# Linear attention fused with its fetch and norm: 64-token scores on array tiles in place of prefix sums

## The reference

```python
# x: (2, 2048, 128); 16 heads of 8 channels
q, k, v = (x @ Wq.T + bq), (x @ Wk.T + bk), (x @ Wv.T + bv)   # split into heads
kv = cumsum(k[..., :, None] * v[..., None, :], axis=tokens)   # an 8x8 state per head
o = einsum("d,de->e", q, kv)                                  # per token and head
x = layernorm(x + o @ Wo.T + bo)
logits = x @ Wr                                               # 8 experts
```

## Time and profile before

| | |
|---|---|
| median of 3 runs | 961.96 us (959.95 to 966.99) |
| span of the profiled execution | 962.4 us |
| fetch, from the first gather, to the start of the attention's own work | 514.8 to 558.0 us |
| attention, first projections and first pieces | 558.0 to 568.9 us |
| attention, from there to its last piece | 568.9 to 697.7 us |
| norm n2 with the router | 697.7 to 729.3 us |

### The profile page before, as it was taken

The page is one execution under the profiler, slowest core; times in us unless marked ns, Lnnn a source line. Parts: engine busy times, 40 slices in busy tenths (PEclk is TensorE's granted clock), DMA queues, the critical chain, the costliest instruction groups (busy, mean ns, idle before and its releaser), DMA issues. The chain is left out here.

```text
span 962.4 us, 32417 instructions
## 1 busy us (share of the span) xinstructions
PE 671.7 (70%) x12441; PEld 475.6 (49%) x12441; DVE 534.8 (56%) x1730; ACT 303.4 (32%) x759; POOL 354.6 (37%) x621
## 2 busy tenths in 40 slices
PE   5776016887876753677780259999853499999991
PEld 4655016777775742576770125444452144545551
DVE  4572611222232386577771039999875757767763
ACT  4453011112211131455561101111131156566551
POOL 3676011111106601333314745555302224554532
PEclk9885555787785776799995559999966599999996
DMA  3000131111108204121111110000001433333430
GB/s 96 8 19 19 49 123 42 49 65 65 66 30 253 79 1 90 26 46 48 46 41 45 52 42 17 16 18 17 11 0 33 84 96 95 109 103 106 103 90 1
DMA packets 61633, 55.36 MB, mean 58 GB/s; under 512 B 12095, under 2 KB 56174, under 8 KB 61296
## 3 DMA queue, kind: packets, MB, share of 16 engines
q1 hardware_dynamic: 56336, 44.48, 15.6%
q0 software_dynamic: 5216, 9.87, 4.8%
HBM read 20.63 MB, written 11.93 MB: 34 GB/s over the span
## 5 line engine op out<-in xcount | busy, mean ns | idle before, releaser
L1134 POOL TENSOR_TENSOR l_kv<-l_qkv 128x512 f32<-128x512 f32 x64 | 71.0, 1131 | 58.0 <-DVE l_qkv L1230 58.0
L1833 PE MATMUL e_psH<-wac,e_xT 128*64 x184 | 90.8, 616 | 0.6 <-ACT e_xT L1893 0.6
L1835 PE MATMUL e_psH<-e_up_w,e_xT 128*64 128x512 f32 x184 | 90.8, 617 | 0.0
L1780 POOL DMA_INDIRECT e_row<-xe_dram,e_read_at x46 | 44.6, 969 | 72.6 <-DVE spare L2020 44.3
L1416 POOL DMA_INDIRECT e_row<-xe_dram,e_read_at x39 | 37.4, 960 | 86.7 <-DVE spare L1584 65.4
L533 POOL TENSOR_TENSOR tb<-tinv,mb 128x128 f32<-128x128 f32 x64 | 24.3, 401 | 113.1 <-PE d_psY L543 113.1
L1171 PE MATMUL l_t<-l_kv,l_tri 128*128 128x512 f32 x128 | 63.9, 621 | 2.9 <-POOL l_kv L1134 1.5
L1785 POOL DMA_INDIRECT out<-spare,e_write_at x46 | 46.4, 1009 | 47.5 <-ACT spare L1910 37.1
L1454 PE MATMUL e_psH<-e_xT,e_up_w 128*128 128x128 f32 x312 | 47.4, 300 | 19.7 <-issue 19.7
L1498 ACT ACTIVATE e_hT<-e_psH,e_b 128x128 f32<-128x128 f32 x156 | 44.7, 373 | 41.4 <-PE e_psH L1454 41.3
L1230 DVE TENSOR_TENSOR l_qkv<-l_a,l_b_qkv 128x384 f32<-128x384 f32 x34 | 19.0, 558 | 64.6 <-PE l_a L1145 63.6
(11 more groups left out here) (342 smaller groups left out, 1916.4 us busy)
## 6 DMA issues: line engine op xcount, KB each, us to landing
e_down_w<-vb SPq DMA_DIRECT2D x92, 128.0 KB, 2.0
xe_dram<-xe SPq DMA_DIRECT2D x2, 2080.0 KB, 12.4
vk_now<-vk SPq DMA_DIRECT2D x16, 192.0 KB
kq_now<-kq SPq DMA_DIRECT2D x16, 192.0 KB
outs_dram<-spare SPq DMA_DIRECT2D x39, 64.0 KB
l_xs<-xT_all SPq DMA_DIRECT2D x34, 64.0 KB, 1.8
r<-in_L_attn_hidden_states SPq DMA_DIRECT2D x8, 256.0 KB, 4.2
gk_now<-gk SPq DMA_DIRECT2D x16, 128.0 KB, 2.0
```

Source lines behind the costliest of these rows:

```text
L1134: pool.tensor_tensor(kv[b][:, i].rearrange("p (h e d) -> p h e d", e=DH, d=DH), k.unsqueeze(2).broadcast_to([P, NH // 2, DH, DH]), spread( ...
L1780: pool.indirect_dma_start(out=row[g % ROWS][:, :], out_offset=None, in_=x_dram, in_offset=bass.IndirectOffsetOnAxis(ap=read_at[:, g:g + 1] ...
L1833: nc.tensor.matmul(psH[g % 2][0:HALF, j], xT[g % 2][:, 0:HALF], wac[:, bass.ds(who[0][j], 1)].rearrange("p a f -> p (a f)"), start=True, s ...
L1835: mm = nc.tensor.matmul(psH[g % 2][HALF:P, j], xT[g % 2][:, HALF:P], up_w[g % 2][j][:, :], start=True, stop=True)
```

## The change

Three stages become one, `stage_attend`. It works on 8 groups of 512 tokens (sequence 0 and 1 in turn), and nothing of it is a loop of the program: all groups are written out.

There are no products k times v per token now. Within 64 tokens, scores are formed as q times k for each of 16 heads, masked to the lower triangle, and multiplied by v. On TensorE a `unit` (L1511) gives the scores of four heads (j) for four pieces of 64 tokens: 4 matmuls on array tiles of 32 rows by 64 columns, 256 columns wide. So that a 32-row tile, which holds four heads, gives the scores of one, GpSimd writes four masked copies of q (`mask_q`, L1439, into `spare`). VectorE masks the scores (L1703). `attend` (L1536, L1544) adds, on tiles of 32 output columns, state times q (16 matmuls) and values times scores (64 matmuls) in one bank; the values lie in `l_vw` padded with zeros, so that each head's window puts its 8 channels in their place. The state of each 64-token piece is a compact 128x32 (L1524, 4 matmuls on 32x32 tiles, kept by VectorE at L1709). Then come output projection (L1555), residual and norm statistics, root and normalising (ScalarE, four times 128x128), a turn of the normed rows (L1561) and the router (L1567, 8 columns in place of 128). Biases of q and k are columns now, since these are computed transposed. GpSimd adds the output bias to the rows (`add_bias`, L1444) and issues the gathers two groups ahead.

```diff
...
+def stage_attend(nc, io, sb, router):
+    NH, C = 16, 64
+    DH, R = D // NH, 4
+    NJ = NH // R
+    SLOTS = 16
+    UNITS, BANKS = 2 * R, 3
+    G = GROUPS
...
+        qT = [tmp(f"qT{i}", [D, 8, C]) for i in range(3)]
+        rooms = [sb["spare"][:, i * 4 * 512:(i + 1) * 4 * 512] for i in range(4)]
+        qm = [t.rearrange("p (c j l) -> p c j l", c=8, j=NJ) for t in rooms[0:2]]
+        vw = [tmp(f"vw{i}", [P, 4, NH + 1, 4 * DH]) for i in range(2)]
+        A = [t.rearrange("p (r k j l) -> p r k j l", r=R, k=2, j=NJ) for t in rooms[2:4]]
+        S = tmp("S", [P, B, SLOTS, NJ * DH])
...
+        psA = [bank(f"psA{i}", [P, 2, NJ * C]) for i in range(BANKS)]
+        psO, psS = bank("psO", [P, 2, 512]), bank("psS", [P, B, NJ * DH])
+        psR = [bank(f"psR{i}", [P, 4, P]) for i in range(2)]
...
+                def gather(g):
+                    for n in range(blocks_of(g).start, blocks_of(g).stop):
                         pool.indirect_dma_start(out=xe[:, n, 0:D], out_offset=None, in_=io["outs0"],
                                                 in_offset=bass.IndirectOffsetOnAxis(ap=slot[:, n:n + 1], axis=0)).then_inc(row_in[g], 16)
+                def mask_q(g):
+                    pool.wait_ge(q_sb, g + 1)
+                    if g >= 2:
+                        pool.wait_ge(a_ps, UNITS * (g - 1))
+                    for j in range(NJ):
+                        pool.tensor_scalar(qm[g % 2][:, :, j], qT[g % 3][:, :, :], of_j[:, j:j + 1], None, ALU.mult).then_inc(qm_done, 1)
+                def add_bias(g):
+                    pool.wait_ge(row_in[g], 64)
+                    pool.wait_ge(x_ps, g + 1)
+                    pool.tensor_tensor(xe_of(g), xe_of(g), b_o[:, :].unsqueeze(1).broadcast_to([P, 4, D]), ALU.add).then_inc(xb_done, 1)
+                gather(0)
...
+                    pool.memset(vw[i][:, :, :, :], 0.0).then_inc(const, 1)
+                pool.memset(S[:, :, 0], 0.0).then_inc(const, 1)
+                gather(1)
+                pool.wait_ge(masks, 2)
+                pool.wait_ge(bo_in, 16)
+                for g in range(G):
+                    if g + 2 < G:
+                        gather(g + 2)
+                    add_bias(g)
+                    mask_q(g)
...
+                def unit(g, pair, r):
+                    n = UNITS * g + R * pair + r
+                    if pair == 0 and r == 0:
+                        pe.wait_ge(qm_done, NJ * (g + 1))
+                        pe.wait_ge(k_sb, g + 1)
+                    if n >= BANKS:
+                        pe.wait_ge(a_sb, n - BANKS + 1)
+                    for k in range(2):
+                        for ch in range(2):
+                            c = 4 * pair + 2 * k + ch
+                            mm = nc.tensor.matmul(psA[n % BANKS][half(ch), k], kT[g % 2][quad(r), 2 * pair + k, half(ch)],
+                                                  qm[g % 2][quad(r), c].rearrange("p j l -> p (j l)"), start=True, stop=True)
+                    mm.then_inc(a_ps, 1)
...
+                def state(g, c):
+                    n = 8 * g + c
+                    if n:
+                        pe.wait_ge(s_sb, n)
+                    k, ch = c // 2, c % 2
+                    for r in range(R):
+                        mm = nc.tensor.matmul(psS[quad(r), g % B], kt[g % 2][half(ch), k, quad(r)], vw[g % 2][half(ch), k, 1 + NJ * r:1 + NJ * r + NJ, 0:DH],
+                                              start=False, stop=True, skip_group_check=True)
+                    mm.then_inc(s_ps, 1)
...
+                def attend(g, pair):
+                    pe.wait_ge(s_sb, 8 * g + 4 * pair + 3)
+                    for k in range(2):
+                        for ch in range(2):
+                            c = 4 * pair + 2 * k + ch
+                            for r in range(R):
+                                nc.tensor.matmul(psO[quad(r), ch, half(2 * pair + k)], S[quad(r), g % B, slot_of(g, c)], qT[g % 3][quad(r), c],
+                                                 start=(pair == 0 and k == 0), stop=False, skip_group_check=True)
+                    pe.wait_ge(a_sb, UNITS * g + R * pair + R)
+                    for k in range(2):
+                        for j in range(NJ):
+                            for r in range(R):
+                                for ch in range(2):
+                                    at = 4 * DH * (1 + NJ * r + j) - DH * j
+                                    mm = nc.tensor.matmul(psO[quad(r), ch, half(2 * pair + k)],
+                                                          vw[g % 2][half(ch), 2 * pair + k].rearrange("p h c -> p (h c)")[:, at:at + 4 * DH],
+                                                          A[pair][half(ch), r, k, j], start=False, stop=(j == NJ - 1), skip_group_check=True)
+                    mm.then_inc(o_ps, 1)
...
+                for g in range(G + 2):
+                    now, ahead, back, far = g < G, g + 1 < G, 1 <= g <= G, g >= 2
+                    if now:
+                        unit(g, 0, 0)
+                    if ahead:
+                        turn_x(g + 1)
+                    if now:
+                        state(g, 0)
+                        unit(g, 0, 1)
+                        state(g, 1)
+                    if ahead:
+                        queries(g + 1)
...
+                        attend(g - 1, 1)
+                    if now:
+                        unit(g, 1, 0)
+                    if far:
+                        route(g - 2)
+                    if now:
...
+                    if back:
+                        output(g - 1)
+                    if now:
+                        attend(g, 0)
...
+            @block.vector
+            def _(dve):
+                v = nc.vector
+                def mask_scores(g, pair, r):
+                    n = UNITS * g + R * pair + r
+                    dve.wait_ge(a_ps, n + 1)
+                    if r == 0 and g:
+                        dve.wait_ge(o_ps, 2 * g + pair - 1)
+                    v.tensor_tensor(A[pair][:, r].rearrange("p k j l -> p (k j) l"), psA[n % BANKS][:, :, :].rearrange("p k (j l) -> p (k j) l", l=C),
+                                    tri[:, :].unsqueeze(1).broadcast_to([P, 2 * NJ, C]), ALU.mult).then_inc(a_sb, 1)
...
         stage_single(nc, io, sb, "e0", w_in, **w)
         give_back(nc, (v_in,))
-        with ExitStack() as attention:
-            sb["xT"] = attention.enter_context(nc.sbuf_tensor("xT_all", [D, B * L], F32))
-            stage_fetch(nc, io, sb, "f0")
-            stage_linear_attention(nc, io, sb)
-            del sb["xT"]
+        stage_attend(nc, io, sb, router[1])
         give_back(nc, (v_in,))
-        stage_norm(nc, io, sb, "n2", router[1])
```

More of the change, by code:

```diff
@@ new lines, in queries, with keys, turn_keys @@
+                def queries(g):
+                    pe.wait_ge(x_sb, g + 1)
+                    nc.tensor.matmul(flat(psR[0][:, :, :]), wT[:, 0], flat(xT[:, :, :]), start=True, stop=True).then_inc(q_ps, 1)
+                def keys(g):
+                    pe.wait_ge(q_sb, g + 1)
+                    nc.tensor.matmul(flat(psR[0][:, :, :]), wT[:, 1], flat(xT[:, :, :]), start=True, stop=True).then_inc(k_ps, 1)
+                def turn_keys(g):
+                    pe.wait_ge(k_sb, g + 1)
+                    if g >= 3:
+                        pe.wait_ge(l_sb, g - 2)
+                    elif g:
+                        pe.wait_ge(kt_sb, g)
+                    for k in range(4):
+                        mm = nc.tensor.transpose(psR[1][:, k], kT[g % 2][:, k], ident[:, :])
+                    mm.then_inc(kt_ps, 1)
@@ new lines, in values @@
+                def values(g):
+                    pe.wait_ge(k_sb, g + 1)
+                    for k in range(4):
+                        mm = nc.tensor.matmul(psR[0][:, k], xT[:, k], wT[:, 2], start=True, stop=True)
+                    mm.then_inc(v_ps, 1)
+                def unit(g, pair, r):
+                    n = UNITS * g + R * pair + r
+                    if pair == 0 and r == 0:
+                        pe.wait_ge(qm_done, NJ * (g + 1))
+                        pe.wait_ge(k_sb, g + 1)
+                    if n >= BANKS:
[6 more added lines that the diff above has]
+                    mm.then_inc(a_ps, 1)
@@ new lines, in output, with turn_normed @@
+                def output(g):
+                    pe.wait_ge(o_sb, g + 1)
+                    pe.wait_ge(kt_sb, min(g + 3, G))
+                    if g:
+                        pe.wait_ge(l_sb, g)
+                    for k in range(4):
+                        mm = nc.tensor.matmul(psR[1][:, k], oT[:, k].rearrange("p c l -> p (c l)"), wT[:, 3], start=True, stop=True)
+                    mm.then_inc(y_ps, 1)
+                def turn_normed(g):
+                    pe.wait_ge(xn_done, 4 * g + 4)
+                    for k in range(4):
+                        mm = nc.tensor.transpose(psR[1][:, k], xe[:, blocks_of(g).start + k, 0:D], ident[:, :])
```

(11 more changed lines are left out.)

420 lines of the change are left out of this document (208 added, 212 removed).

## The result

The changed kernel takes 1006.3 us (1001.6 to 1008.8) against 964.5 for the kernel before, measured beside it: a ratio of 1.045, with an interval of 1.040 to 1.050. The forecast was 989, range 942 to 1014, slower with 0.57.

What follows compares the result with a forecast made beforehand. The prediction took TensorE as the bound, at 20.7 us per group. A region of 204.1 us against 214.2 gave 952; plus 28 for code-loading stops and 9 for half clock made 989, range 942 to 1014.

Steps and rivals of the forecast that it cites:

- the region without stops: Whole replaced region, first gather to last logits, without further stalls: 204.1 us against 214.2 before, giving 952.
- Stops of code loading: In attend's small tiles, instruction loads stop TensorE 16 times at 1.75 us: 28 us, bounds 16 and 30.
- each of the two bursts holds a load, whatever the phase: Attend's 160 records, twice per group, exceed the 132 matmuls per load, so each was counted as one stop.
- The clock: In the groups, half clock after some stops costs TensorE 9 us; none 0, all 27.
- a third of 16 stops: In attend, this share of stops is followed by 3.4 us at half clock: 5 x 1.7 = 9 us.
- rows 10: Earlier trace: after TensorE worked 1.66 of 3.5 us at 0.99, the next 3.4 us ran at 0.51.
- the clock falls for good: Rival: stops and switches bring the groups' clock to 0.8, total 1005 to 1040; chance 0.12.
- TensorE in a group: TensorE's work per group of 512 tokens sums to 20.7 us, against 16.1 before.
- The rival that the array packs better: Cheaper shape changes, overlapping units or nearly free route make the region 25 us shorter: 920 to 945; chance 0.16.
- Prologue: First gather to first unit, waiting on GpSimd for masked q of group 0: 25.3 us, bounds 24 to 27.
- VectorE's answers: Rival: TensorE waits for masked states in each group, adding 20 to 30 us, about 980; no chance of its own.
- Stops hidden: Rival: instruction loads are fetched ahead without stopping TensorE, total 952 (945 to 962); chance 0.22.

Runs made afterwards that it cites:

- the run with 128 rows: Changed kernel with score units reading all 128 rows instead of 32, so each score sums four heads: 963.2 us, ratio 1.003 to the kernel before.
- The runs with one, two and four bursts: Changed kernel with zero-padded keys, masked queries issued earlier, memsets on VectorE, and attend in one, two or four pieces per group: ratios to the kernel before 1.007, 0.989, 0.988.
- the other prologue: Changed kernel with masked queries issued ahead of later gathers and bias addition, and memsets moved from GpSimd to VectorE: median 1005.8 us, no ratio.

## Why the prediction was right, and where it was not

The sign and the range were right (+4.5% measured, +2.8% forecast); the ground given was wrong in its main part. Two terms were mis-sized in opposite directions, stops by 23 us too much and the clock by some 35 too little, and that they cancelled enough for 1006 to lie in the range is luck. The rest of the sum held: 204.1 us were forecast for the region without stops, and the run with 128 rows has 214.2 with 5.3 us of stops and 1.9 of a longer prologue in it, which leaves 2.9.

**Stops of code loading** (16 x 1.75 = 28 us): measured 4 and 5.2 us, of a bound of 16 to 30. The count of loads was right (31 against "some 30"); a stop was shorter than the 1.75 taken (0.8 to 1.7 us idle, 1.3 on the mean). The step that failed is "each of the two bursts holds a load, whatever the phase", taken to mean that each stops. Twelve of the 16 bursts hold the start of one, and only four stop. What counts is how much of the burst is left when the load starts: behind the stop before 577.05 us it starts at 574.6, with some 80 records still running before TensorE stands still. A load that starts later in a burst has units behind it and is hidden. The runs with one, two and four bursts (12, 5 and 2 stops) bear it out.

**The clock** (9 us, at most 27): this was the loss. Some 43 of 45 us hang on it, as the run with 128 rows shows at once. The step that failed is the price of a third of 16 stops: the clock fell without stops, and did not fall with them where the units had 128 rows. I had put a third of 16 stops at half clock on the strength of rows 10 and held the rest of the group to be safe because most of it "is work on large tiles, which ran at 1.0". The units are 6.9 of 20.7 us by the forecast, and three quarters of the rows are idle in them; I priced them by the time of a column and never asked how many rows they fill. Of the rivals, "the clock falls for good" came nearest (0.8 forecast for it, 0.72 measured); it had a chance of 0.12 and the wrong trigger, stops and switches. Its 1005 to 1040 with the stops on top meets the measured 1006 only because most of the stops weren't there.

**TensorE in a group** (20.7 us): right. The group period at full clock with no stop is 21.1 in the run with 128 rows and 20.7 in the window of the other prologue. The pitch of units (0.21 a record pair), small tiles, and 0.15 for a change of shape held as a sum; they were not tested one by one. The rival that the array packs better is out: no group from 2 to 6, which have all their parts, ran under 20.7.

**Prologue** (25.3, bounds 24 to 27): 27.2. The masked copies at 1.56 take 3.0 us more than forecast and the constants 0.9 less. The bound was wrong, as a copy from one source was taken to be no dearer than a product of two.

**VectorE's answers**: TensorE waited 1.1 us in all for a masked state, so that rival is out too. **Stops hidden** was nearer to the truth of the stops than the forecast, and would have been wrong on the time by 54 us. The rule of the Trainium skill, page "Runtime: NRT & Kernel Launch", section "Instruction fetch mechanics", that crossing a block is mostly hidden agrees with the trace after (27 of 31 loads didn't stop L1544), and less where small tiles run for 320 records (12 stops of 1.6 us on the mean).

## What to carry to other kernels

Price a small tile by the rows it fills too, not only by its columns: a long row of tiles that fill a quarter of the rows took TensorE to half clock here, and one operand padded with zeros to 128 rows, against 128 rows of the other, gave it back at no time of its own. The changes of tile shape are the easy suspect and were not the cause: 193 us became 150 with as many of them. When a loop is written out, look for the longest row of short instructions and not only at the size of the code: with 0.8 us or more of other work between four bursts of 80 records, two stops were left, 1.6 us in all, where one burst of 320 has twelve and 18.6.

## What was not expected

Rows in which one operand holds zeros keep the clock up as rows with data in both do (0.97 either way). Zeros in both were not tried. Whether it is the rows of the loaded weights or of the moving operand stays open: both went from 32 to 128 together. With a tenth of TensorE's work left out, the kernel became slower (1023.8 us, clock 0.58). A masked copy of 128x512 with a column as scalar takes GpSimd 1.56 us, while a product of two such tiles takes 1.13 and the addition at L1444 1.18.
